# Layer 0 of a four-layer transformer kernel: attention scores by single heads in two row tiles of TensorE, maxima by DMA, and elementwise work moved from GpSimd to VectorE

## The reference, cut to what matters

```python
q, k = rope(xn @ wq), rope(xn @ wk)                     # heads of 16
scores = einsum('bnth,bnsh->bnts', q, k) / sqrt(16)
scores = where(causal, scores, -inf)
out = einsum('bnts,bnsh->bnth', softmax(scores), v)     # then @ wo
W = (w4 - (z4 + 1)) * scale                             # dequantised 4-bit weights
h = silu(xn @ Wg) * (xn @ Wu);  ffn = h @ Wd
```

## Time and profile before

| | |
|---|---|
| median of 3 runs | 2556.29 us (2554.38 to 2558.05) |
| profiled execution, its own time | 2561.34 us |
| its span | 2559.6 us |
| mean granted TensorE clock | 0.983 of full |
| busy: TensorE, VectorE, ScalarE, GpSimd | 2455.2, 1618.1, 1102.4, 618.3 us |

### The profile page before, as it was taken

One profiled execution on the slowest core, in us unless ns is written; L12 is line 12 of the kernel. 1 busy time (PEld: TensorE's weight loads), 2 busy tenths in 40 slices (PEclk: granted clock), 3 DMA queues, 4 the chain that ended last, 5 costly groups with the idle time before them and its releaser, 6 DMA issues. The chain is left out here.

```text
span 2559.6 us, 40914 instructions
## 1 busy us (share of the span) xinstructions
PE 2455.2 (96%) x14448; PEld 1962.8 (77%) x14448; DVE 1618.1 (63%) x2388; ACT 1102.4 (43%) x2158; POOL 618.3 (24%) x455
## 2 busy tenths in 40 slices
PE   5989999999989989999999999999999999999899
PEld 4767777778866668888888878888888877888666
DVE  5886567864477776545444467777777776543576
ACT  3322145443255533223333366666666653323453
POOL 3343110246321226124444400000000024430100
PEclk8999999999989999999999999999999999999999
DMA  2232164122332212234444332222222222322421
GB/s 86 62 101 83 52 122 88 31 38 43 57 89 59 48 28 42 45 98 140 148 148 143 125 114 87 83 90 90 68 75 86 66 44 39 53 46 33 102 63 37
DMA packets 406207, 195.33 MB, mean 76 GB/s; under 512 B 280393, under 2 KB 359729, under 8 KB 406079
## 3 DMA queue, kind: packets, MB, share of 16 engines
q1 hardware_dynamic: 404860, 191.53, 30.0%
q10 hardware_dynamic: 1218, 2.06, 0.3%
HBM read 129.85 MB, written 44.04 MB: 68 GB/s over the span
## 5 line engine op out<-in xcount | busy, mean ns | idle before, releaser
L603 PE MATMUL banks<-xn_hi,w_hi 128*128 128x512 f32 x1264 | 496.6, 393 | 12.9 <-ACT sgf L1146 10.0
L603 PE MATMUL banks<-xn_lo,w_hi 128*128 128x512 f32 x1264 | 493.1, 390 | 0.0
L603 PE MATMUL banks<-xn_hi,w_lo 128*128 128x512 f32 x1264 | 492.9, 390 | 0.0
L603 PEld LDWEIGHTS banks<-xn_hi,w_hi 128*128 128x128 f32 x1264 | 238.0, 188 | 64.4 <-DVE w_lo L591 10.4
L603 PEld LDWEIGHTS banks<-xn_hi,w_lo 128*128 128x128 f32 x1264 | 237.9, 188 | 49.7
L603 PEld LDWEIGHTS banks<-xn_lo,w_hi 128*128 128x128 f32 x1264 | 238.1, 188 | 48.4
L591 DVE TENSOR_TENSOR w_lo<-tw,w_hi 128x512 fp32r<-128x512 f32 (+2 forms) x136 | 117.0, 867 | 201.8 <-ACT w_hi L583 201.7
L2719 DVE TENSOR_SCALAR raw<-banks,cols 128x512 f32<-128x512 f32 x128 | 103.7, 810 | 180.3 <-ACT sq L2702 180.3
L2731 POOL TENSOR_TENSOR ssq<-ssq,sq 128x512 f32<-128x512 f32 x128 | 165.1, 1290 | 183.2 <-ACT sq L2702 183.2
L469 POOL TENSOR_TENSOR nat<-nat,wscale 128x512 f32<-128x512 f32 (+1 forms) x44 | 51.5, 1179 | 651.6 <-DMA nat<-in_L_ffn_w 651.4
L1258 POOL TENSOR_TENSOR h_lo<-sgf,h_hi 128x512 fp32r<-128x512 f32 (+1 forms) x94 | 128.1, 1367 | 288.8 <-ACT h_hi L1149 288.8
(11 more groups left out here) (302 smaller groups left out, 5831.5 us busy)
## 6 DMA issues: line engine op xcount, KB each, us to landing
qk_scratch<-raw SPq DMA_DIRECT2D x64, 512.0 KB, 3.0
qk_raw<-qk_scratch SPq DMA_DIRECT2D x64, 512.0 KB, 3.8
nat<-in_L_ffn_w SPq DMA_DIRECT2D x48, 256.0 KB
head_scratch<-stage SPq DMA_DIRECT2D x16, 512.0 KB, 3.2
st_qs<-st_hi SPq DMA_DIRECT2D x128, 64.0 KB, 2.1
nat<-in_L_attn_Wq SPq DMA_DIRECT2D x32, 256.0 KB
nat<-in_L_attn_Wk SPq DMA_DIRECT2D x32, 256.0 KB
nat<-in_L_attn_Wv SPq DMA_DIRECT2D x32, 256.0 KB
```

The lines of the kernel that those rows point to most:

```text
L603: mm = nc.tensor.matmul(to[half][:, :], w[0:n, j, k * P:(k + 1) * P], r, start=first and k == 0 and x == 0, stop=last and k == len(rows) - ...
```

## The change

In layer 0's attention every head is a score of its own. A head needs 48 rows (hi, lo, hi against hi, hi, lo, of 16) and 4 rows for the shift, and stands in one of two row tiles of 64 rows: four heads of a chunk in rows 0 to 63, four in rows 64 to 127. Every matmul of a score or shift part uses one tile; the parts are cut so that all heads of a part are in the same tile, and `both` issues a score part of one chunk and a shift part of another, in the other tile, alternating matmul by matmul. The causal mask comes from two matmuls of 64 rows (`square`, `row64`, made from constants which SP loads in `sp_v0`). The maxima of all heads are copied by ScalarE to `neg_tops` (8 rows), and two DMAs on ScalarE's own queue carry them to the query rows (`copy_tops`), with a semaphore `tops_in` for even and odd chunks. Key buffers need no zeros, so GpSimd's clearing of them goes; the rows of -1 are written in two parts for a unit and signalled for each unit, and SP loads a unit by 12 DMAs. Two more loops on TensorE change their order: the half of the values of the first key block is moved between the steps (`values(i, kb, e)`).

Outside it: `dve_unpack` is cut out of `dve_dequant` and runs for the next chunk before the low part of this one; the cosine product of the rotary embedding goes from GpSimd to VectorE; the low parts of all norms are made by VectorE alone; and the first down chunk is loaded, spread, unpacked and rounded before the last chunk of the up products (`down_ahead`, `pe_down_ahead`).

```diff
+        def score_heads(part):
+            return (0, part, 0, PAIRS) if part < 2 else (1, part % 2, 2 * (part // 2 - 1), 2)
+        def shift_heads(part):
+            return (0, part % 2, 2 * (part // 2), 2) if part < PAIRS else (1, part % 2, 0, PAIRS)
+            def both(i, part, j, part2):
...
+                    if n >= 3:
+                        pe.wait_ge(max_done.sem, s.mx + n - 2)
...
+                    if m >= 2:
+                        pe.wait_ge(exp_done.sem, s.ex + m - 1)
+                    if part2 == 0:
+                        pe.wait_ge(tops_in[j % 2].sem, s.ti[j % 2] + 32 * (j // 2 + 1))
...
+                for b in range(2):
+                    if here:
+                        nc.tensor.matmul(o[:, :, qt * P + b * ROW_TILE:qt * P + (b + 1) * ROW_TILE], square[tile(e, ROW_TILE), 0, b, :],
+                                         bcast(row64[tile(e, ROW_TILE), :], n_p), start=b == 0, stop=False, skip_group_check=True)
+                    if there:
+                        nc.tensor.matmul(o2[:, :, b * ROW_TILE:(b + 1) * ROW_TILE], square[tile(e2, ROW_TILE), 1, b, :],
+                                         bcast(row64[tile(e2, ROW_TILE), :], n_p2), start=b == 0, stop=False, skip_group_check=True)
+                for x in range(PAIRS):
+                    if here and x < n_p:
+                        mm = nc.tensor.matmul(o[:, x, :], q[tile(e, TERMS), p + x, qt * P:(qt + 1) * P], k[tile(e, TERMS), p + x, 0:keys],
+                                              start=False, stop=x == n_p - 1, skip_group_check=True)
...
+                    if there and x < n_p2:
+                        mm = nc.tensor.matmul(o2[:, x, :], k2[tile(e2, TERMS + PAIRS), p2_ + x, kb * P:(kb + 1) * P],
+                                              q2[tile(e2, TERMS + PAIRS), p2_ + x, kb * P:SEQ],
+                                              start=False, stop=x == n_p2 - 1, skip_group_check=True)
...
+            for i in range(-3, CHUNKS):
+                for n in range(3):
+                    both(i + 2, 3 + n, i + 1, n)
+                values(i, 0, 0)
+                tops(i + 2)
+                for n in range(2):
+                    both(i + 3, n, i + 1, 3 + n)
+                values(i, 0, 1)
+                values(i, 1, 0)
+                values(i, 1, 1)
+                both(i + 3, 2, i + 1, 5)
...
+            def copy_tops(i):
...
+                act.wait_ge(top_turned.sem, s.tt + i + 1)
+                nc.scalar.activation(neg_tops[0:HPC, i % 2, :], bank[5][0:HPC, i % 2 * SEQ:(i % 2 + 1) * SEQ], ACT.Copy)\
+                  .then_inc(top_copied.sem, 1)
+                act.wait_ge(top_copied.sem, s.tc + i + 1)
+                slot = att_place(s, i)[2]
+                for e in range(2):
+                    row = e * ROW_TILE + TERMS
+                    act.dma_start(unit_qs[slot][row:row + PAIRS, :, i % 2 * SEQ:(i % 2 + 1) * SEQ].bitcast(F32),
+                                  bcast(neg_tops[e * PAIRS:(e + 1) * PAIRS, i % 2, :].bitcast(F32), PAIRS)).then_inc(tops_in[i % 2].sem, 16)
...
+            for i in range(-3, CHUNKS + 2):
+                for part in range(3):
+                    exps(i + 1, part)
+                copy_tops(i + 2)
+                high_part(i - 2)
+                for part in range(3, STEPS):
+                    exps(i + 1, part)
...
+            for i in range(-3, CHUNKS + 1):
+                for part in range(3, STEPS):
+                    top(i + 2, part)
...
+                inverse(i - 1)
+                top(i + 3, 0)
+                norm(i - 1)
+                for part in range(1, 3):
+                    top(i + 3, part)
```

```diff
             ins.then_inc(dequant.sem, 1)
+            if i + 1 < s.n:
+                dve_unpack(dve, s, i + 1, (i + 1) % SLOTS, parts_of(s, i + 1))
+            dve_lo(dve, s, i, j, parts)
...
+            def down_ahead(left):
+                if left == 1:
+                    dve_unpack(dve, s.then, 0, 0, parts_of(s.then, 0))
+                    dve_dequant(dve, s.then, 0, 0, parts_of(s.then, 0))
...
                 dve.wait_ge(step_a.sem, s.a0 + n + 1)
+                nc.vector.tensor_tensor(seqs(v), seqs(v), bcast(cst[:, C_COS0:C_COS0 + SEQ], 2), ALU.mult).then_inc(step_c.sem, 1)
                 nc.vector.tensor_tensor(seqs(rot), seqs(rot), bcast(cst[:, C_SIN0:C_SIN0 + SEQ], 2), ALU.mult)\
...
         def dve_low_x(dve, s, half):
-            for k in range(0, KT, 2):
-                low_x(dve, nc.vector, s, half, k)
-
-        def pool_low_x(pool, s, half):
-            for k in range(1, KT, 2):
-                low_x(pool, nc.gpsimd, s, half, k)
+            for k in range(KT):
+                low_x(dve, s, half, k)
...
+                for e in range(2):
+                    rows = slice(e * ROW_TILE + QUAD, (e + 1) * ROW_TILE)
+                    ins = nc.vector.tensor_copy(stacks[rows, :, :], tail_bcast(cst[rows, C_NEG1:C_NEG1 + PAIRS], HALF))
+                ins.then_inc(shift_rows.sem, 1)
...
-            for stacks in unit_ks:
-                nc.gpsimd.memset(stacks[0:ROWS, :, :, :].bitcast(F32), 0.0).then_inc(slot_clear.sem, 1)
```

More of the change, by code:

```diff
@@ L61 @@
 C_MASK = 384
+C_NEG1 = 512
 C_COS0, C_SIN0, C_COS1, C_SIN1 = 520, 776, 1032, 1288
@@ L540, in dve_dequant @@
             ins.then_inc(unpacked.sem, 1)
+        def dve_dequant(dve, s, i, j, parts):
             dve.wait_ge(unpacked.sem, s.un0 + i + 1)
@@ L1141, in ahead @@
                     pe_up_delta(pe, s, i, j, ft)
-            up_rounds(pe, s, ahead, work, opening, lead=LEAD - 1 if s.behind else LEAD_TURN, first=first, seam=seam_pe(pe, s))
+            def down_ahead(left):
+                if left == 1:
+                    pe_down_ahead(pe, s.then, 0)
+            up_rounds(pe, s, ahead, work, opening, lead=LEAD - 1 if s.behind else LEAD_TURN, first=first,
+                      seam=down_ahead if s.then else seam_pe(pe, s))
         def act_gate(act, s, half):
@@ L1248, in work, with down_ahead @@
                     dve_gated(dve, s, half)
-            up_rounds(dve, s, ahead, work, opening, LEAD if s.tw is None else LEAD_TURN, first, pair, 1, seam_dve(dve, s))
+            def down_ahead(left):
+                if left == 1:
+                    dve_unpack(dve, s.then, 0, 0, parts_of(s.then, 0))
+                    dve_dequant(dve, s.then, 0, 0, parts_of(s.then, 0))
+            up_rounds(dve, s, ahead, work, opening, LEAD if s.tw is None else LEAD_TURN, first, pair, 1,
+                      down_ahead if s.then else seam_dve(dve, s))
         def pool_up_scale(pool, s, i, j, ft):
@@ L1375, in proj_order @@
         def proj_order(s, ahead, work, opening, lead=LEAD, seam=None):
-            for i in range(min(lead, s.n)) if opening else ():
+            for i in range(1 if s.up and s.up.then is s else 0, min(lead, s.n)) if opening else ():
                 ahead(i, i % SLOTS, s.chunks[i])
@@ L1389, in load, with pe_down_ahead @@
             def load(i, j, c):
-                sp_slot(sp, s, i)
+                if s.up and s.up.then is s and i < SLOTS:
+                    sp.wait_ge(centred.sem, s.up.cen0 + s.up.n - (s.up.n - 1 - i) % SLOTS)
+                else:
+                    sp_slot(sp, s, i)
                 for dst, src in c["loads"]:
                     sp.dma_start(dst(j), src).then_inc(loaded[j].sem, 16)
+            if opening and s.up and s.up.then is s:
+                load(0, 0, s.chunks[0])
             proj_order(s, load, lambda i, j, c: None, opening, LEAD_LOAD)
+        def pe_down_ahead(pe, s, i):
+            c = s.chunks[i]
+            pe_spread(pe, s, i, i % SLOTS, [HOT["down"] + kt * P for kt in c["kts"]], c["cols"])
         def pe_chunk_delta(pe, s, i):
@@ L1402, in ahead @@
                 if s.mode == "dequant":
-                    pe_spread(pe, s, i, j, [HOT["down"] + kt * P for kt in c["kts"]], c["cols"])
+                    pe_down_ahead(pe, s, i)
                 elif s.adapters:
@@ L2007, in pool_pair @@
         def pool_pair(pool, s, ft):
-            for n in rotated(ft):
-                pool_piece(pool, s, n)
             for n in rotated(ft - 2, 1):
@@ new lines, in unit_load @@
+        def unit_load(sp, s, u, kind, e):
+            half, c = divmod(u, QC)
+            slot = u % UNIT_SLOTS
+            src = head_dram["kq".index(kind), c, :, :, :, at(half)].rearrange("j r x t -> r j x t")[e * HD:(e + 1) * HD]
+            for x, part in enumerate((0, 0, 1) if kind == "k" else (0, 1, 0)):
+                rows = slice(e * ROW_TILE + x * HD, e * ROW_TILE + (x + 1) * HD)
+                sp.dma_start((unit_ks if kind == "k" else unit_qs)[slot][rows, :, :].bitcast(F32), src[:, :, part, :])\
+                  .then_inc(unit_in[slot].sem, 16)
@@ new lines, in sp_units, with sp_att0 @@
+        def sp_units(sp, s):
+            for j in range(SLOTS):
+                sp.wait_ge(stage_out[j].sem, in0.st0[j] + 16 * len(PIECES) // SLOTS)
+            for u in range(UNIT_SLOTS):
```

(10 more changed lines are left out.)

234 lines of the change are left out of this document (173 added, 61 removed).

## The result

The changed kernel takes **2593.5 us** (median of 4 runs, 2586.8 to 2602.3), the kernel before 2556.8 (4 runs beside it, 2554.4 to 2558.1). The ratio is 1.0147, with a 95% interval of 1.0114 to 1.018: slower by 37 us, where I forecast 32 us faster. The profiled execution took 2602.3 us (span 2600.5), against 2561.3 (span 2559.6) before.

What follows compares the result with a forecast made beforehand. TensorE, busy 96% of the span, was taken as the bound. Attention 16, gate and up 9, seam 5 and norms 2 sum to 32 us: 2529 for the profiled execution, 2524 us for the median, range 2510 to 2547.

Steps and rivals of the forecast that it cites:

- the maxima's way: Layer 0's attention: maxima go by ScalarE copy and DMA, landing at 6.4 to 8.4 us, needed at 7.4, just hidden.
- Rival B: Attention: the maxima's DMA sets the pace, landing 4.1 us after issue; period 8.7 us, total 2542 us; chance 0.12.
- the units' buffers: Before attention: units' first loads start up to 4.7 us later, same bytes; cost 0, at worst 3 us.
- the first chunk's way: Start of attention: nothing hides the first chunk's maxima, transposes, copy and DMA; 1 to 4 us more, taken as 2.
- The products: Attention: paired row tiles overlap, a pair costing its longer half, 0.35 or 0.62 us; 2.9 to 3.2 us a chunk.
- Rivals A: Attention: weight loads of the two tiles go one after another; pairs cost 4.2 us, total 2536 us; chance 0.22.
- C: Attention: row tiles don't run together; 5.8 us for the parts, period 10.2 us, total 2564 us; chance 0.09.
- D: Attention: VectorE's 6.2 us and short waits become the bound, period 6.7 us, total 2512 us; chance 0.07.
- The run-up: Start of attention, before the steady periods: 2 us more, for the first chunk's maxima that nothing hides.
- Gate and up products: Layer 0's gate and up: early unpacking and the moved cosine product cut TensorE's waits; +9 us, bounds +2 and +11.
- The seam: From up to down products: the first down chunk, prepared early, removes TensorE's wait; +5 us, bounds 0 and +5.5.
- Low parts of the norms: All norms: VectorE alone makes four per half, each faster than when shared; +2 us, bounds -3 and +4.

Runs made afterwards that it cites:

- paced: Changed kernel, same bytes: two units loaded up front, later ones in lots of 4, 6 and 2 loads after a chunk's maxima land, output weights after units; 2569.4 us.
- ordered: As reordered, with the 19 small loads of biases and columns issued after the last unit's loads; 2542.9 us, ratio 0.9935.
- turned order: Shifted scores of a chunk moved half a period later, giving the maxima's DMA more slack; alone on the changed kernel 2565.3 us.
- reordered_filled: As reordered, with 48 extra products into a bank nobody reads, in the gaps of the run-up; 2548.8 us, ratio 0.9975.
- rest_no_low: As rest_only, but the norms' low parts shared between VectorE and GpSimd as before; 2548.8 us, ratio 0.9972.
- rest_only: Kernel before with every edit of the change except the new attention; 2551.4 us, ratio 0.998.
- quarter_loads: Changed kernel, but from the fourth unit on each load brings a quarter of the bytes (scores wrong, a probe); 2558.6 us.
- reordered: Changed kernel with turned order, four unit buffers, half of unit 2 up front, earlier lots of six, small loads moved, adapter transposes spread, norms as before; 2546.5 us.
- ordered_filled: As ordered, with 16 extra products into an unread bank, one per gap of the run-up; 2548.5 us, ratio 0.9954.

## Why the prediction was wrong, step by step

**The step that failed is "the maxima's way"**: I took the DMA "as just hidden in most chunks" from landings of 2.1 and 4.1 us, which are of another stage. I had written that the DMA share of 0.40 is a mean and that a unit's loads fall in every second chunk, and that is the pattern that cost the time, but I priced it at 2 us in all. Rival B is this mechanism, undersized: 4.1 us of landing in every chunk, where it was 7.5 us in one of two. A round trip that is put on the critical path has to be priced with the queue at its fullest, and the trace of the kernel before had it. Its units' loads in the attention itself (340 to 480 us; KB each, median us to landing) took longer than what I used:

```profile
qs<-head_scratch SPq DMA_DIRECT2D x15, 256.0 KB, 4.8
ks<-head_scratch SPq DMA_DIRECT2D x30, 128.0 KB, 6.5
```

In the changed kernel it is more: twelve loads of 128 KB at the 135 GB/s of 333 to 340 us, where the DMA engines are full, are 11.7 us. I had also put the new loads down as "the same bytes". Where the three units are loaded, the DMA engines moved 191 GB/s at a share of 0.95 before (313.93 to 330 us) and 130 GB/s at 0.99 in the changed kernel (313.82 to 331.80), so the same bytes kept them busy longer; no run tests that apart. The Trainium skill, "DMA: Bandwidth & Descriptors", says under "Issuing engines are not separate DMA queues" that DMAs of the scalar and sync engines run on the same 16 DMA engines and interleave. The 7.5 us agree with it: a queue of their own didn't keep the maxima's landing short beside SP's loads.

The same step failed at the start of the stage. I put the units' buffers at 0, "at worst 3 us", and the first chunk's way at 2; behind 36 loads and the first of the output weights the first chunk waited 11.5 us, and in paced, with 24 loads ahead and the output weights' last, that wait is gone.

**What the wait sets off** was missing from every case of mine. The granted clock was at 0.50 from 335.6 to 366.3, and after that seven more times for 3 to 10 us (403.8 to 410.7 beside the wait shown), so that it was at 0.83 in the mean of 380 to 420 us. The long wait didn't begin this: the clock fell five us before it, after 2.3 us of the stage in which TensorE had worked 1.90 (the stretches of 333.21 and 336.00 above), and it fell in the same place in ordered (334.5 to 355.0), which has no such wait. What the 11.5 us did, at most, is to keep it low for longer. TensorE's busy time in the stage is 139.6 us; at full clock ordered needs 73.16/11 = 6.65 us a period, 106 for sixteen. So the stage's 43 us (142.8 to 186.0) come out as an estimate: the new products save 138.4 - 106 = 32 us of TensorE's work, the low clock takes 139.6 - 106 = 33 back, and standing still grew from 4.4 to 46 us.

**The products** were right. In ordered at full clock, a pair of two-head parts and the start of the next:

```profile
376.83 0.23 PE L2376 MATMUL banks<-row,square 64*128 64x128 bf16 x1
376.83 0.23 PE L2379 MATMUL banks<-row,square 64*128 64x128 bf16 x1
...
376.92 0.36 PE L2383 MATMUL banks<-ks,qs 48*128 48x256 f32 x1
376.93 0.36 PE L2388 MATMUL banks<-qs,ks 52*128 52x256 f32 x1
...
377.25 0.23 PE L2376 MATMUL banks<-row,square 64*128 64x128 bf16 x1
```

0.42 us (I said 0.35); a pair of a four-head and a two-head part takes 0.64 us (378.21 to 378.85; I said 0.62). Three of each are 3.2 us, the upper end of my 2.9 to 3.2. Rivals A (4.2) and C (5.8) are out. The period came out at 7.2 us in the changed kernel, 7.0 at best in the turned order, against 7.4. As the Trainium skill has it ("TensorEngine Tiling (Array Packing)", Key Properties), changing the mode drains TensorE; my estimate with a drain of 0.28 us was 8.3 us, and the periods of 7.0 and 7.2 us speak for the small switch of the earlier trace rows. In the turned order VectorE is the next floor, as in D: it works 68.19/11 = 6.2 us of each period.

**The run-up** I gave 2 us. Before, 142.8 us were fifteen periods of 8.73 and 11.8 us; in ordered 131.2 are fifteen of 7.28 and 22.0: 10 us more, with the clock at 0.71 over the first 35 us. The low clock alone isn't the reason: in reordered_filled it stayed at 1.00 and the fifth copy came no sooner. The turned order adds half a period of this by its construction. The rest is open. By these numbers it is the run-up that keeps ordered at -14 us in place of some -24 (an estimate).

**Gate and up products**: right in size. Unpacking takes 0.49 us everywhere (0.96 before in the mean), TensorE's waits up to the last up product fell from 10.0 to 7.1 us in the trace of the changed kernel and to 4.4 in that of rest_no_low (I said 2.5), and the edits bring about 7 us by the medians (I said 9).

**The seam**: +5 became 0 to 2.4. My step missed when the load comes. Of rest_no_low:

```profile
232.29 0.42 DVE L539 TENSOR_SCALAR nat<-nat,shift 128x384 int32<-128x384 int32 x1 [8.23 <-DMA nat<-in_L_ffn_down_qweight]
...
234.95 1.28 DVE L1211 TENSOR_TENSOR sgf<-sgf,banks 128x512 f32<-128x512 f32 x2
...
236.73 0.55 DVE L556 TENSOR_TENSOR deq<-deq,banks 128x384 f32<-128x384 f32 x1
...
237.34 0.39 PE L530 MATMUL banks<-table,hot 128*128 128x256 bf16 x2 [2.69 <-DVE deq L556]
```

VectorE stands still for 8.2 us, blocked by the load of the first down chunk, while TensorE finishes; both gate products of the last tile queue behind, and so does the second chunk's dequantising, for which TensorE then waits. I had named the queueing ("1 to 2 us late; TensorE doesn't need them at once") and missed that the second chunk stands behind them.

**Low parts of the norms**: +2 was nothing, or a small loss. TensorE waited for them 3.1 us in 6 places before, 3.5 in 3 in rest_only and 3.2 in 6 in rest_no_low: fewer waits, but longer ones. With four on VectorE in a row, the last of them meets GpSimd's sum and is late: in rest_only

```profile
502.49 2.36 DVE L910 TENSOR_TENSOR xn_lo<-cen,xn_hi 128x512 fp32r<-128x512 f32 x2
502.65 1.65 POOL L844 TENSOR_TENSOR ln_sum<-ln_sum,xT 128x512 f32<-128x512 f32 x1 [4.72 <-DVE xT L1354]
504.91 0.50 PE L1095 MATMUL banks<-xn_lo,w_hi 128*128 128x512 f32 x1 [1.18 <-DVE xn_lo L910]
```

One of the four took 1.76 us where the others take 0.68, and TensorE waits 1.18 us where its longest wait was 0.5. I had the low parts of before slow because both engines made them at a time; here GpSimd makes its sum beside them, and the low part is slow again.

## What to carry to other kernels

Before a DMA is put between two engines' work, price its landing behind the largest burst that any queue issues in that stage, not by a row of another stage, and give it that much slack in the order of the work; here half a period of slack was worth 28 us and the order of the loads 24, each without touching a byte. Here a wait on TensorE cost itself and, mostly, the clock behind it, so a sum of waits was a lower bound. An operation issued ahead on an in-order engine is only ahead if its load has landed; otherwise all that stands behind it is late.

## What the runs showed of the hardware

- Loads of 128 KB landed in 4.8 us (keys) and 7.7 us (queries, the second six of a burst) in the changed kernel, those of 32 KB in 1.9 and 2.0 us in quarter_loads. The DMA of the maxima, 16 KB on another engine's queue, took 7.5 us from the end of its issue in the middle of such a burst.
- Products of the two row tiles of 64 rows start 0 to 10 ns apart at full clock in the rows of ordered above, and their weight loads at the same times, when their instructions stand in turn: 0.42 us for a pair of parts that take 0.35 us alone.
- 48 filling products held the granted clock at 1.00 over 340 to 360 us (reordered_filled), where without them it was 0.62 (reordered); 16 didn't (0.50 there in ordered_filled).
- The granted clock fell to 0.50 some 2.4 us (changed kernel) and 3.5 us (ordered) after the start of the attention stage, where TensorE had stood still for 0.4 and 0.6 us in short pauses; in the kernel before it stayed at 1.00 there.
